# A layernorm–attention–mixture kernel on Trainium2: GpSimd makes all low parts of queries and keys in the projection

## The reference

```python
xn = (x - mean(x)) / sqrt(var(x) + 1e-5)                    # layernorm over the 256 features
q, k, v = split(xn @ Wqkv, 3)                               # 16 heads of 16
Q, K = rope(q), rope(k)
attn = softmax(where(causal, Q @ K.T * 16**-0.5, -inf)) @ V @ Wout + bout
p = softmax(xn @ gate_w.T + gate_b)                         # 10 gates, 8 true experts
weights, selected = top_k(p, 2)                             # normalised over the true ones
ffn = sum over the selected true experts e of weight * (xn @ expert_w[e] + expert_b[e])
return x + attn + ffn
```

## Time and profile before

| what | value |
|---|---|
| three runs | 998.33, 1004.48, 1005.53 us (median 1004.48) |
| profiled execution: span | 1022.0 us |
| `project`, to the last VectorE instruction | 133.5 us of the span |
| PE busy over the span | 907.5 us (89%) |
| DVE busy | 847.0 us (83%) |
| ACT busy | 728.5 us (71%) |
| POOL busy | 462.9 us (45%) |

### The profile page before, as it was taken

The page is one execution under the profiler, slowest core; times in us unless marked ns, Lnnn a source line. Parts: engine busy times, 40 slices in busy tenths (PEclk is TensorE's granted clock), DMA queues, the critical chain, the costliest instruction groups (busy, mean ns, idle before and its releaser), DMA issues. The chain is left out here.

```text
span 1022.0 us, 22104 instructions
## 1 busy us (share of the span) xinstructions
PE 907.5 (89%) x7874; PEld 392.7 (38%) x7874; DVE 847.0 (83%) x1096; ACT 728.5 (71%) x1542; POOL 462.9 (45%) x588
## 2 busy tenths in 40 slices
PE   2888446999999999999999899999999999999888
PEld 1554311332432334344434444344434333322257
DVE  6999789899899878886889688877888799894846
ACT  3556200788788878787888788778878788789822
POOL 4677568565201253344833474354132245355610
PEclk8999755999999999999999999999999999999979
DMA  9766810301200324244413542255334321112113
GB/s 324 267 248 248 276 46 11 105 3 38 68 2 2 115 78 121 76 133 147 125 53 98 151 143 74 72 162 132 77 85 125 90 62 49 32 58 64 37 52 124
DMA packets 82084, 106.65 MB, mean 104 GB/s; under 512 B 10000, under 2 KB 59064, under 8 KB 80952
## 3 DMA queue, kind: packets, MB, share of 16 engines
q1 hardware_dynamic: 74488, 85.83, 26.1%
q0 software_dynamic: 6528, 17.83, 6.8%
q10 hardware_dynamic: 960, 1.57, 0.5%
HBM read 67.37 MB, written 37.50 MB: 103 GB/s over the span
## 5 line engine op out<-in xcount | busy, mean ns | idle before, releaser
L1275 DVE TENSOR_REDUCE blk<-psP 128x2 f32<-128x1024 f32 (+2 forms) x576 | 641.4, 1162 | 103.5 <-PE psP L1421 53.7
L1221 ACT ACTIVATE probs<-psS 128x512 f32<-128x512 f32 (+3 forms) x1280 | 589.2, 541 | 162.2 <-PE psS L1458 153.1
L1458 PE MATMUL psS<-Qs,Ks 50*128 50x512 f16 (+3 forms) x1280 | 332.0, 353 | 24.5 <-ACT probs L1221 15.4
L1418 PE MATMUL psP<-Ks,Qs 48*128 48x512 f16 (+3 forms) x1280 | 299.6, 363 | 31.7 <-DVE blk L1275 20.5
L1514 PE MATMUL psO<-probs,Vs 128*32 128x512 f32 (+3 forms) x2560 | 300.3, 547 | 6.0 <-POOL probs L1124 4.9
L1124 POOL TENSOR_SCALAR_AFFINE_SELECT probs<-probs 128x512 f32<-128x512 f32 x128 | 88.1, 689 | 356.3 <-ACT probs L1221 317.4
L1458 PEld LDWEIGHTS psS<-Qs,Ks 50*128 50x128 f16 x1280 | 96.4, 93 | 256.6 <-ACT probs L1221 149.2
L1418 PEld LDWEIGHTS psP<-Ks,Qs 48*128 48x128 f16 x1280 | 80.4, 94 | 132.9 <-DVE blk L1275 94.8
L1421 PE MATMUL psP<-later,eye 64*128 64x128 bf16 x1024 | 103.6, 223 | 0.0
L1514 PEld LDWEIGHTS psO<-probs,Vs 128*32 128x32 f32 x2560 | 52.9, 108 | 86.4 <-issue 65.2
L1421 PEld LDWEIGHTS psP<-later,eye 64*128 64x128 bf16 x1024 | 78.1, 98 | 19.6 <-issue 1.7
(11 more groups left out here) (170 smaller groups left out, 729.3 us busy)
## 6 DMA issues: line engine op xcount, KB each, us to landing
xn<-we_scratch SPq DMA_DIRECT2D x72, 256.0 KB
expert_scratch<-xn SPq DMA_DIRECT2D x36, 256.0 KB
v_scratch<-vst SPq DMA_DIRECT2D x8, 1024.0 KB, 4.0
qk_scratch<-part SPq DMA_DIRECT2D x32, 256.0 KB, 4.0
Vs<-v_scratch SPq DMA_DIRECT2D x16, 512.0 KB, 3.9
Qs<-qk_scratch SPq DMA_DIRECT2D x168, 32.0 KB
Ks<-qk_scratch SPq DMA_DIRECT2D x168, 32.0 KB
acc<-x SPq DMA_DIRECT2D x8, 512.0 KB, 9.2
```

Source lines behind the costliest of these rows:

```text
L1221: nc.scalar.activation(probs[u % NPR][:, h, q0:CH], psS[:, k % SB, q0:CH], ACT.Exp, scale=exp_scale).then_inc(s_read[k % SB], 1)
L1275: nc.vector.tensor_reduce(out, src, AX.X, ALU.max).then_inc(item_ok[slot], 1)
L1418: ins = pe.matmul(psP[:, slot, at:at + w], Qs[r][rows, qt // CT, p, t * P:(t + 1) * P], Ks[r][rows, kc, p, 0:w], start=True, stop=True)
L1458: pe.matmul(psS[:, k % SB, q0:CH], Ks[r][rows, kt // CT, p, kt % CT * P:(kt % CT + 1) * P], Qs[r][rows, c, p, q0:CH], start=True, stop=Tru ...
```

## The change

In `project`, GpSimd makes the low parts for all four k (two more `low` per pass, behind the two it had), and VectorE's `split` is gone. With that come new orders. On ScalarE the high parts 2 and 3 of a pass, which stood at the head of the next pass, now stand behind `copy_v` of their own pass, and `normal_x` is cut in two halves of two instructions, behind one of them each; `high_x` comes first in a pass. On VectorE, from the second pass on, `norm_a` moves from behind rope 2 to behind rope 1, `norm_c` from behind rope 3 to ahead of it, and `low_e` of the pass before from behind rope 2 to behind rope 3. TensorE's and SyncE's lists are the same.

```diff
@@ GpSimd
                         nc.gpsimd.tensor_tensor(rot[k0 + 1], rot[k0 + 1], turn[k0][:, 1, :], ALU.add
                                                 ).then_inc(sum_ok[k0 + 1], 1)
                         low(s, k0)
+                        low(s, k0 + 1)
@@ ScalarE
-            def normal_x(s, j, b):
-                act.wait_ge(less_ok, ONE + s + 1)
-                for t in range(CT):
+            def normal_x(s, j, b, some=range(CT)):
+                if some[0] == 0:
+                    act.wait_ge(less_ok, ONE + s + 1)
+                for t in some:
...
-                ins.then_inc(xn_ok, 1)
+                if some[-1] == CT - 1:
+                    ins.then_inc(xn_ok, 1)
...
-                    if not first:
-                        high(s - 1, 2)
-                        high(s - 1, 3)
                     if more:
                         high_x(s + 1, 1 - b)
                     high(s, 0)
...
                     high(s, 1)
                     copy_v(s, j, b)
+                    high(s, 2)
                     if not last:
-                        normal_x(s + 2, j + 1, b)
+                        normal_x(s + 2, j + 1, b, range(CT // 2))
+                    high(s, 3)
+                    if not last:
+                        normal_x(s + 2, j + 1, b, range(CT // 2, CT))
                     high_e(s)
...
-            high(LAST, 2)
-            high(LAST, 3)
@@ VectorE
-            def split(s, k):
-                dve.wait_ge(high_ok[k], ONE + s + 1)
-                nc.vector.tensor_tensor(part[k][:, 1, :], rot[k], part[k][:, 0, :], ALU.subtract
-                                        ).then_inc(split_ok[k], 1)
...
                     rope(s, j, 0)
                     rope(s, j, 1)
-                    if not first:
-                        split(s - 1, 3)
+                    if not last and not first:
+                        dve.wait_ge(x_in[s + 2], 16)
+                        norm_a(s + 2, j + 1, b)
                     if first:
                         scale_e()
                     if more:
                         low_x(s + 1, 1 - b)
                     rope(s, j, 2)
+                    if first:
+                        dve.wait_ge(x_in[s + 2], 16)
+                        norm_a(s + 2, j + 1, b)
+                        rope(s, j, 3)
+                    if not last:
+                        norm_c(s + 2, b)
+                    if not first:
+                        rope(s, j, 3)
                     if not first:
                         low_e(s - 1)
-                    if not last:
-                        dve.wait_ge(x_in[s + 2], 16)
-                        norm_a(s + 2, j + 1, b)
-                    rope(s, j, 3)
-                    if not last:
-                        norm_c(s + 2, b)
-                    split(s, 1)
...
-            split(LAST, 3)
```

## The result

The changed kernel takes 1008.7 us (median of 15 runs, 1001.8 to 1012.4) against 1004.48 us before (15 runs): the ratio is 1.0047, 95% interval 1.0027 to 1.0067, so 2.7 to 6.7 us longer. That is within 1%, as forecast, and inside the range, but the likeliest time, 1005, was 3.7 us too low. So the 17.5 us lie behind `project`, and its rows in `project` can be compared.

The account below looks back on a forecast made before the run. VectorE was taken to be full and to bound a pass of 11.4 us. The terms -2.0, -1.8, +5.2 and -0.7 sum to +0.7, so 1004.48 becomes 1005.2, written as 1005 us; the range is 997 to 1012.

Parts of the forecast that it names:

- the 17.5 us: Whole profiled execution before the change: its span of 1022.0 us was 17.5 us more than the median of 1004.48.
- the forecast's own upper bound of 1008: Forecast's slow end in `project`: rounds of 11.4 us and a tail of 19.4 us give 1008 us.
- the logits end: Sign at the end of `project`: the end of L637 would lie within 2 us of 114.6.
- `low_e` is stretched beside GpSimd: Sign in the passes: L491 and `low_e` on VectorE would be stretched beside GpSimd, 0 to 1.23 us each.
- Step 1: Start of `project` to rope 3 of pass 2: it would come at 53.8 where it was 55.82, -2.0 us.
- Step 2: Rope 3 of pass 2 to that of pass 6: three rounds of 10.7 and one of 9.9, 42.0 us, -1.8.
- the ring from TensorE over ScalarE: Within a pass: values, copy, two high parts, `normal_x`, transposes, queries 2 and 3, values again, about 10.0 us.
- The faster rival: Passes and tail: four stores land a microsecond earlier, rings of 10.0 and 9.9 us set the pass; 1001 us, chance 0.22.
- The slower rival: L491 and `low_e`: GpSimd's turn-taking takes more than VectorE saved, rounds of 12.6 us; 1011 us, chance 0.15.
- the two waits: L491 and `low_e` in the ring through the stores: each waits 0 to 1.23 us for GpSimd, 0.6 taken for both.
- Step 3: End of rope 3 of pass 6 to the end of L637: 19.0 us where it was 13.8, +5.2.
- Step 4: Between L637 and the routing: the last `split`, at 114.55, is gone, -0.7 us.

Follow-up runs that it names:

- half the low parts: Changed kernel with GpSimd's `low` on 256 of the 512 columns, the other half of each low part zero: ratio 0.9984 to the kernel before.
- the stores' new order: Changed kernel with SyncE issuing values, part 0 and part 1 ahead of the expert's store of the pass before and the rows: ratio 1.0037 to before.
- the rows first: Changed kernel with ScalarE's four rows of `normal_x` right behind `copy_v` in all passes, high parts 2 and 3 behind them: ratio 1.0018 to before.
- the edit in the first pass: Changed kernel with `normal_x` whole right behind `copy_v` in the first pass alone, high parts 2 and 3 behind it: ratio 1.0035 to before.
- the loads early: Changed kernel with ScalarE's 24 loads of the first heads' keys and queries ahead of the exponent of the gate logits: ratio 1.0021 to before.

## Why the prediction was right, and where not

The rounds came out as forecast. The time also stayed in the range, but there luck had a part: the range had 3.6 us of spread on both ends, the median lies 0.7 us above the forecast's own upper bound of 1008, and what lifted it (the run-in and the loads) is not what that bound stood for (rounds of 11.4). Of the signs named beforehand two failed: the logits end at 117.8 and not within 2 us of 114.6, and `low_e` is stretched beside GpSimd only in pass 6 and behind the last pass, not in the rounds.

*Step 1, to rope 3 of pass 2: forecast -2.0, measured +0.5 (56.28).* This is the term that was mis-sized most. The end of `normal_x`, 39.4, was right to 0.2 us. But I took the products behind it at 2.60 us, a duration from a row at the full clock, although the sum itself left TensorE idle for over 3 us ahead of them; they took 4.38 at the lower clock, and rope 0 of pass 2 came at 49.16 and not 47.2. From there to rope 3 it took 7.1 us and not 6.6: L493 took 0.58 us beside GpSimd's low part 0 where it takes 0.16 alone, and the two ropes 2.56 where they had 2.36.

*Step 2, the rounds: forecast 42.0 us, measured 42.3* (from 56.28 to 98.6, where rope 3 of pass 6 begins). Right in size and in mechanism as far as it went: burst of stores, DMA wait of high part 0, one turn of waiting for GpSimd (L493 0.56 us longer, `low_e` none; I had taken 0.6 for both), and no bound by the length of GpSimd's list, as half the low parts showed. Two things differ inside that sum. The way from high part 0 to rope 3 goes over GpSimd's low part 0, whose end L493 waits out, and not over `deviation`; it costs 0.6 + 1.2 us to rope 3, where I had 0.6, 0.3, 0.2 and a wait of 0.6, so the equal size is in part luck. And this wait is not a random point of an instruction: high part 0 starts the low part, and in each of the four rounds from 55 to 90 us L493 took 0.58 to 0.74 us. It is no semaphore that holds it, as it has started (77.17) and then lasts longer, though I wrote that the engines meet only at semaphores. The Trainium skill (page "SBUF — State Buffer", section "Who interferes with whom") has a VectorE instruction with two SBUF inputs wait for the whole of a GpSimd instruction that reads SBUF; L493's 0.72 us agrees, and so do its 0.16 to 0.25 in the kernel with half the low parts, where low part 0 has ended by then or ends with it. Incomplete in one point: the ring from TensorE over ScalarE was costed at 10.0 and took 11.1 at the full clock with the stores' new order, since high part 2 waits for GpSimd's difference, which waits for rope 3, and L502 for GpSimd. The faster rival, "the stores keep up", was made in the experiment on SyncE's order. Its 1001 us did not come, as that ring stood behind it. The slower rival did not occur: the two waits stayed under its 1.3 us.

*Step 3, rope 3 of pass 6 to the logits: forecast 19.0, measured 17.9* (99.85, where that rope ends, to 117.78; before 13.8). Right: `low_e` behind `high_e` behind high part 3, and a wait of 0.53 us for GpSimd in the `low_e` of pass 6 (1.27 us) where I took 0.6. The logits' three instructions took 1.54 us (116.24 to 117.78) where I had 2.91, since GpSimd was done with its low parts at 115.8.

*Step 4, the last `split`: forecast -0.7.* Between the logits and the routing 0.4 us are gone (0.1 us from 117.78 to 117.89, 0.5 before), but the routing itself took 0.4 us longer, so VectorE's end moved by as much as the logits.

*What I costed at nothing.* "Behind it the list of the attention is the same" was true and not enough: the stage also ends with 24 loads, which ended 4 to 5 us ahead of VectorE before. In the changed kernel they took 7 us longer and became the last to end: 3 us more in the first product, shown by issuing them early. The sum had no term for what else ends the stage. Without the loads the stage would have ended 3.1 us later where the sum had 0.7: step 1 alone is 2.5 us of that difference, and the other steps nearly cancel.

## What to carry to other kernels

When work is taken off a full engine, list all rings through the other engines and cost each with its waits, not only with its instructions; two rings of about the same length hide each other, and an experiment that cuts one can look like a refutation. If a sum leaves TensorE idle for some us (here 2 us and more), cost what follows at the lower clock as well. And before a tail is costed, look at what else ends the stage, above all loads ahead for the next one.

## What the runs showed of the hardware

Behind the transposes' waits for `normal_x`, over all kernels here, the twelve query products took 2.75 us when the wait was up to 1.98 us, and 3.4 to 4.7 when it was 2.07 to 3.69; once they took 2.75 behind 2.24, so the length of the wait alone does not tell which. With the rows first they took 3.51 once without such a wait, behind one of 3.50 us ahead of query 1 (68.36). The packets of the 24 loads, 960 and 1.57 MB in all, took twice as long in the changed kernel as before. The page's lines on their queue, changed kernel and before (the last figure is the time of their packets as a share of 16 engines' span):

```profile
q10 hardware_dynamic: 960, 1.57, 1.0%
```

```profile
q10 hardware_dynamic: 960, 1.57, 0.5%
```

With the edit in the first pass it was 1.0% too, with the loads early 0.4 and 0.5%, elsewhere 0.5 to 0.7%. The two at 1.0% are those in which the stores of the last pass ended soonest after the loads began, but no run here tells why, and it stays open.
